# A dynamic convolution on one core: the low halves of the inputs subtracted on GpSimd instead of VectorE

## The reference

```
def _gn(v, G=32, eps=1e-05):            # groups of 2 channels
    ...
    return ((g - m) / jnp.sqrt(s + eps)).reshape(v.shape)

pooled = x.mean(axis=(2, 3))            # x is _gn of the input here
a = relu(pooled @ fc1_w.T + fc1_b)
att = softmax(a @ fc2_w.T + fc2_b)      # 4 numbers an image
agg_w = einsum('bk,koihw->boihw', att, weight)
agg_b = att @ bias
out = conv 3x3, padding 1, of each image with its own agg_w
return x + out + agg_b                   # x is the input, not normalised
```

## Time and profile before

| | |
|---|---|
| Times of three runs | 334.3, 334.58 (median), 336.71 us |
| Profiled execution | 337.77 us, of which the span is 336.0 us |
| TensorE (PE) | busy 301.9 us, 90% of the span |
| VectorE (DVE) | 216.5 us, 64% |
| ScalarE (ACT) | 198.4 us, 59% |
| GpSimd (POOL) | 73.2 us, 22% |
| TensorE's mean granted clock | 0.984 of full speed |

### The profile page before, as it was taken

The page is one execution under the profiler, slowest core; times in us unless marked ns, Lnnn a source line. Parts: engine busy times, 40 slices in busy tenths (PEclk is TensorE's granted clock), DMA queues, the critical chain, the costliest instruction groups (busy, mean ns, idle before and its releaser), DMA issues.

```text
span 336.0 us, 15462 instructions
## 1 busy us (share of the span) xinstructions
PE 301.9 (90%) x6996; PEld 268.9 (80%) x6996; DVE 216.5 (64%) x482; ACT 198.4 (59%) x258; POOL 73.2 (22%) x291
## 2 busy tenths in 40 slices
PE   0059939999899999999998999999999999999993
PEld 0048836977799889999776899888998799999993
DVE  3469669498849494967759394958769494628000
ACT  1062582888293957667582948567584849395221
POOL 3400630407430404031220404040220304000000
PEclk9998996999999999999999999999999999999999
DMA  8980500939484755748282856548392506070554
GB/s 247 290 370 2 197 0 4 257 132 230 158 227 162 198 190 152 236 100 268 66 274 74 203 188 179 207 106 272 66 289 69 175 5 194 4 188 9 131 162 98
DMA packets 14306, 53.61 MB, mean 160 GB/s; under 512 B 6816, under 2 KB 7968, under 8 KB 12192
## 3 DMA queue, kind: packets, MB, share of 16 engines
q1 hardware_dynamic: 14240, 52.62, 52.6%
HBM read 26.89 MB, written 25.69 MB: 156 GB/s over the span
## 4 chain that ended last, share of the span: by engine, by line
PE 78%; DVE 8%; DMA 3%; ACT 3%; POOL 3%; issue 3%; SPq 1%; ACTq 0%; DVEq 0%
PE acc L509 78%; DMA w_sb<-w_t 3%; DVE mix L333 2%; DVE xl L355 2%; ACT x L402 2%; DVE stats L294 1%; DVE wpart L372 1%; POOL gm L267 1%; POOL sums L271 1%; SPq L196 0%; DVE wl L346 0%; PE tiny L496 0%; DVE mix L331 0%; ACT xh L409 0%; ACT o L445 0%
## 5 line engine op out<-in xcount | busy, mean ns | idle before, releaser
L509 PE MATMUL acc<-xh,wh 64*64 64x392 f16 x2304 | 124.3, 335 | 9.5 <-ACT wh L423 7.8
L445 ACT ACTIVATE o<-acc,out_par 128x392 f32<-128x392 f32 x128 | 79.5, 672 | 86.0 <-PE acc L509 85.6
L509 PE MATMUL acc<-xh,wl 64*64 64x392 f16 x2304 | 122.0, 330 | 0.4 <-DVE xl L355 0.3
L509 PE MATMUL acc<-xl,wh 64*64 64x392 f16 x2304 | 120.5, 327 | 0.0
L509 PEld LDWEIGHTS acc<-xh,wh 64*64 64x64 f16 x2304 | 94.8, 108 | 20.1 <-ACT wh L423 5.7
L509 PEld LDWEIGHTS acc<-xh,wl 64*64 64x64 f16 x2304 | 94.8, 107 | 10.7 <-issue 1.4
L509 PEld LDWEIGHTS acc<-xl,wh 64*64 64x64 f16 x2304 | 94.1, 106 | 9.6
L294 DVE BATCH_NORM_STATS2 stats<-x 128x6 f32<-128x448 f32 x112 | 60.7, 611 | 5.0 <-DMA x<-x 5.0
L355 DVE TENSOR_TENSOR xl<-x,xh 128x1568 f16<-128x1568 f32 x32 | 57.2, 1790 | 0.9 <-ACT x L402 0.8
L402 ACT ACTIVATE x<-x,xof,xsc 128x1568 f32<-128x1568 f32 x32 | 53.9, 1686 | 0.4
L409 ACT ACTIVATE xh<-x 128x1568 f16<-128x1568 f32 x30 | 45.2, 1507 | 0.5
(11 more groups left out here) (52 smaller groups left out, 123.4 us busy)
## 6 DMA issues: line engine op xcount, KB each, us to landing
x<-x SPq DMA_DIRECT2D x15, 1568.0 KB, 10.9
out<-o SPq DMA_DIRECT2D x60, 392.0 KB, 5.2
out<-o SPq DMA_DIRECT2D x16, 98.0 KB, 2.2
x<-x SPq DMA_DIRECT2D x3, 448.0 KB, 4.4
w_sb<-w_t SPq DMA_DIRECT2D x2, 576.0 KB, 9.6
out_par<-par SPq DMA_DIRECT2D x64, 0.5 KB, 2.1
x<-x SPq DMA_DIRECT2D x1, 224.0 KB, 7.1
small_sb<-small SPq DMA_DIRECT2D x1, 16.0 KB, 6.9
```

The lines of the kernel that those rows point to most:

```text
L445: nc.scalar.activation(o_sb[i][m][:, g * GN:(g + 1) * GN], acc[n % SLOTS][m][:, 0:GN], ACT.Identity, bias=out_par[i][m][:, 1:2], scale=out ...
L509: ins = nc.tensor.matmul(acc[n % SLOTS][m][halves[r], 0:GN].rearrange("p (r c) -> p r c", c=W), weights[i][halves[m], tap * C:(tap + 1) * ...
```

## The change

The two subtractions that make `xl` go from VectorE's order to GpSimd's. GpSimd does them for pair p+1 behind its chain for pair p+2; for pair 0, ahead of its chain for pair 1. The waits before each subtraction stay as they were, and so do data, types and the operation. VectorE's order closes up.

```diff
-            for p in range(PAIRS):
-                group_stats(p)
+            def low_inputs(p, half):
+                i = p % 2
+                pool.wait_ge(s_xn, 2 * p + half + 1)
+                pool.wait_ge(s_xh, 2 * p + half + 1)
+                if p >= 2:
+                    pool.wait_ge(s_conv, 2 * GROUPS * (p - 1))
+                nc.gpsimd.tensor_tensor(inner(xl[i], half), rows_of(x_sb[p % X_RING], half),
+                                        inner(xh[i], half), ALU.subtract).then_inc(s_xl, 1)
+
+            group_stats(0)
+            low_inputs(0, 0)
+            low_inputs(0, 1)
+            group_stats(1)
+            for p in range(PAIRS - 1):
+                if p + 2 < PAIRS:
+                    group_stats(p + 2)
+                low_inputs(p + 1, 0)
+                low_inputs(p + 1, 1)
...
-            low_inputs(0, 0)
-            low_inputs(0, 1)
             params(0)
             channel_stats(1)
...
                 mixture(p + 1)
-                low_inputs(p + 1, 0)
                 low_weights(p + 1)
-                low_inputs(p + 1, 1)
                 params(p + 1)
```

More of the change, by code:

```diff
@@ L347, in low_weights @@
                                                op0=ALU.mult, op1=ALU.subtract).then_inc(s_wl, 1)
[L349 to L356, removed]
             def params(p):
```

## The result

The changed kernel takes 345.0 us (median of 4 runs) against 335.45: ratio 1.0315, 95% interval 1.0266 to 1.0365 (estimated from all runs; the quotient of the two medians, 1.0285, lies inside it). Slower, as forecast, by half of the +19 us that was forecast. The profiled execution took 348.0 us, its span 346.2 against 336.0.

The account below looks back on a forecast made before the run. TensorE was taken as the bound, its products without a break in the steady part, VectorE setting no time there. Terms 2.1 + 6.2 + 4.2 + 8 - 1.3 = +19 on 334.6 gave 353.6 us, range 335 to 371.

Parts of the forecast that it names:

- The hold: GpSimd reads and VectorE two-input instructions exclude each other for a whole instruction, in both directions; chance 0.62.
- (a): Rival: GpSimd yields, pausing for VectorE, which is never held; +4, 338.3 us; chance 0.17.
- (b): Rival: no mutual hold for these accesses; +0.6, 335 us; chance 0.14.
- L = 3.4 us: Time of one subtraction on GpSimd, taken as the middle between 2.7 (two steps an element) and 4.0 (three).
- Pair 0, +2.1: TensorE waits 2.1 us for xl, ready on GpSimd at 32.9 us, before pair 0's low products.
- Pair 1, +6.2: Both xl halves hold the mixture, wh comes at 58.6 against 50.0 us; total shift 8.3, so +6.2 more.
- Pair 2, +4.2: Held mixture delays wh and the group 1 results behind it: 83.8 against 79.5 us.
- -1.3: Gain: TensorE's 1.31 us wait at 86 us for the statistics of pair 4 goes.
- Steady, +8: Over 13 pairs, one in three loses 1.8 us, 0.6 a pair: +8, the least certain term.
- the steps: Steady-part reckoning of successive periods: mv's arrival at GpSimd decides whether xl's halves fall inside the mixture.
- The room: Steady part: wh may end at 17.0 us of the period instead of 11.7, 5.3 us for 6.8 of GpSimd.
- the assumed turns: Under the hold, a waiting instruction of either engine goes in as the other's instruction ends.

Follow-up runs that it names:

- the fastest version: Pairs 3 to 15 and half of pair 0 on GpSimd, ScalarE reordered at pair 1, image sums sooner, against the kernel before: 330.63 us, ratio 0.9857.

## Why the prediction was right, and where not

**The hold: right.** It was argued from one long row in the other direction and one of 0.04 us. The trace after shows it both ways, for one instruction at a time: at pair 1 for VectorE, and where a short instruction of GpSimd meets the mixture (`gm` at 239.81 took 0.81 us instead of 0.26). Rivals (a) and (b) are out, since `att` and the first step of pair 1 took 3 us each. What a hold adds is 2.7 us there, a little less than GpSimd's 3.06.

**L = 3.4 us: somewhat high.** It is 3.06 where GpSimd is alone, 1.83 ns an element: nearer to two steps of the memset's 0.81 than to three.

**Pair 0, +2.1: 1.4 measured**, which is 26.1 + 6.1 - 30.8. **Pair 1, +6.2: the wait grew by 5.5**, right for this L; the path by about 4.1 (5.2 in the table, less pair 0's 1.4 and plus 0.4 us by which this execution started sooner). The difference is the 0.27 us for xl, foreseen, and the clock, which came back 1 us sooner behind the longer wait (0.99 from 59.6 to 62.7 us, where before had 0.72 from 53.2 to 57.5): the low products of the first group took 3.0 us (59.63 to 62.67) and not 4.1. Not foreseen. **Pair 2, +4.2: 4.5 measured**, and the nearness is luck. The wait, at the place and by the order foreseen, was 2.2; the low clock behind it, not foreseen, added 1.6; the last 0.7 I did not trace, 0.3 of it idle of TensorE with no releaser. **-1.3: right.**

**Steady, +8: this failed.** It is nil by the runs with pairs 3 to 15 alone on GpSimd; in this one trace 1.9, of which 1.2 is more idle of TensorE with no releaser (3.1 in all against 1.9). In the steps mv wanders from 4 to 5.4 to 2.8 us of a period, and the loss, 1.8 us, was at 2.8. That case exists, about as often as forecast: in three of the eleven pairs 3 to 13 both halves come before the mixture's end. The pair that starts at 99.3, with mv at 2.8:

```profile
107.36 8.03 DVE L349 SCALAR_TENSOR_TENSOR mix<-w_sb,att,mix 128x576 f32<-128x576 f32 x3
...
108.19 6.59 POOL L280 TENSOR_TENSOR xl<-x,xh 128x1568 f16<-128x1568 f32 x2
...
115.74 0.78 ACT L426 ACTIVATE wh<-mix,wsc 128x576 f16<-128x576 f32 x1 [6.95 <-DVE mix L354]
```

The mixture took 8.9 us (106.80 to 115.70) and not 10.2, since a hold adds 2.7 and not 3.4, and wh ended at 17.2, not 18.8. The room ends at 17.0, so the case costs 0.2 us, by which this pair was longer than 18.24 (18.42 from sums to sums). The step that failed is this price: 1.8 us was put on it, and 0.2 was measured.

Most of the others fit with room, like the pair that starts at 231.4:

```profile
235.21 0.15 DVE L319 STREAM_SHUFFLE mv_other<-mv 128x2 f32<-128x2 f32 x1
```

```profile
242.24 3.19 DVE L354 SCALAR_TENSOR_TENSOR mix<-eye,std,mix 128x64 f32<-128x64 f32 x1
242.29 6.07 POOL L280 TENSOR_TENSOR xl<-x,xh 128x1568 f16<-128x1568 f32 x2
...
246.27 2.71 DVE L362 SCALAR_TENSOR_TENSOR wl<-mix,wsc,wh 128x576 f16<-128x576 f32 x1 [0.84 <-ACT wh L426]
...
248.97 0.15 DVE L372 TENSOR_TENSOR bprod<-att,small_sb 128x4 f32<-128x4 f32 x1
```

```profile
253.62 0.15 DVE L319 STREAM_SHUFFLE mv_other<-mv 128x2 f32<-128x2 f32 x1
```

The start is reckoned from the pair's sums at 245.1, less three quarters of a period. mv comes at 3.8, xl takes 10.9 to 17.0, meeting only the eye matrix and wl; params follows at 17.6, unheld, and mv comes again 18.4 us after the last. So it reproduces itself, with 2.8 us to spare for xl. By the same reckoning mv stood between 1.9 and 4.4 in pairs 3 to 9 and at 3.8 or 3.9 in pairs 10 to 13. The steps had params wait for the second half behind wl, and mv thus drift to 5.4; here wl waits for that half and params follows unheld. What the wrong 0.3 us of L and what the assumed turns did to the forecast, no run separates. The size of the whole was off by this term: 19 - 8 = 11, and 9.6 was measured.

**Open.** Why a GpSimd instruction sometimes takes 3.57 instead of 3.06 us was read only as its wait for VectorE at the start; TensorE's idle times with no releaser; whether GpSimd's share is worth anything in the fastest version's later pairs; why `tensor_scalar` on one element isn't held.

## What to carry to other kernels

Moving work from VectorE to GpSimd is no relief for VectorE's other instructions unless they are of a kind that isn't held: here the statistics, with one input, were of that kind, two-input operations and float32 `tensor_scalar` on 4 or 576 elements were not. Price a move by the work on the receiver and by one hold for each instruction that it issues, and only where somebody waits: the same move cost 3% at three pairs, and nothing at thirteen. Where a chain of short instructions must go by, cut the long one into pieces, or put it beside something that isn't held.

## What the runs showed of the hardware that was not expected

A memset on GpSimd, which reads nothing, stretched a float32 `tensor_scalar` on VectorE from 0.5 to 3.4 us and left two-input instructions at 819 ns. VectorE's eye matrix, started 0.05 us ahead of GpSimd's subtraction (242.24 and 242.29), still waited for it (3.19 us instead of 0.28): the start that the profile shows does not decide who comes first. TensorE's clock fell to a mean of 0.64 behind a wait of 2.2 us at pair 2 and stayed at 1.00 behind one of 0.5; behind pair 1 it was back sooner after 10.8 us of idle than after 5.3.
